# Six layers on one Trainium2 core: X transposes over two slots in the attentions, P^T kv in P's banks, expert slots in order of expert

## The reference

```python
x = norm(x + L0_attn(x))    # "gqa": rope over heads, 16 q heads, 4 kv heads, softmax, biases
x = norm(x + L0_xattn(x))   # "latent": 16 heads, scores over a 128-wide latent context
x = norm(x + L0_ffn(x))     # ternary weights, 512 -> 1408 -> 512, sigmoid gate
x = norm(x + L1_attn(x))    # "decay": linear attention in blocks, 16 heads, biases
x = norm(x + L1_xattn(x))   # "causal": keys and values from the 128-wide context, softmax
x = norm(x + L1_ffn(x))     # 8 experts, two chosen per token, and a shared expert

# L1_ffn
logits = x @ gate_weight.T
topk_w, topk_idx = top_k(softmax(logits), 2)
y[t] = sum over the two experts e of t:  topk_w * (down_e @ (silu(g) * u)),  (g, u) = gate_up_e @ x[t]
y += shared expert
```

## Time and profile before

| | |
|---|---|
| runs, median (lowest to highest) | 2352.07 us (2348.92 to 2352.67) |
| profiled execution, its own time | 2348.88 us |
| its span in the trace | 2347.1 us |
| mean granted clock of TensorE | 0.93 |
| busy: TensorE / DVE / ACT / POOL | 2015.7 / 1078.3 / 711.8 / 356.7 us |
| from the last expert matmul to the end | 70.6 us |

### The profile page before, as it was taken

One profiled execution on the slowest core, in us unless ns is written; L12 is line 12 of the kernel. 1 busy time (PEld: TensorE's weight loads), 2 busy tenths in 40 slices (PEclk: granted clock), 3 DMA queues, 4 the chain that ended last, 5 costly groups with the idle time before them and its releaser, 6 DMA issues. The chain is left out here.

```text
span 2347.1 us, 32879 instructions
## 1 busy us (share of the span) xinstructions
PE 2015.7 (86%) x12204; PEld 1636.4 (70%) x12204; DVE 1078.3 (46%) x1916; ACT 711.8 (30%) x2261; POOL 356.7 (15%) x317
## 2 busy tenths in 40 slices
PE   4899958889999978999789996899977999899970
PEld 3777636777777756777667774677756777799960
DVE  4466743344444436433344454566754232222226
ACT  1455623233333333111131101344532121233322
POOL 0111000000000007300021100000002300544216
PEclk9899968999999998999889997899987999999995
DMA  5011133000000004000150001000013200543226
GB/s 176 1 38 38 39 120 121 31 1 1 1 1 1 1 1 135 14 0 0 40 216 1 1 1 63 1 1 1 1 40 112 108 0 0 209 146 133 82 74 190
DMA packets 54284, 125.65 MB, mean 54 GB/s; under 512 B 5248, under 2 KB 23040, under 8 KB 51840
## 3 DMA queue, kind: packets, MB, share of 16 engines
q1 hardware_dynamic: 29088, 83.91, 10.2%
q0 software_dynamic: 5840, 27.92, 3.4%
q10 hardware_dynamic: 19216, 11.89, 1.8%
HBM read 90.68 MB, written 33.03 MB: 53 GB/s over the span
## 5 line engine op out<-in xcount | busy, mean ns | idle before, releaser
L1165 PE MATMUL banks<-ternary_xth,ternary_wq 128*128 (+1 forms) x352 | 138.5, 393 | 1.4 <-DVE ternary_xtl L73 1.4
L1165 PE MATMUL banks<-ternary_xtl,ternary_wq 128*128 (+1 forms) x352 | 138.3, 393 | 0.0
L388 ACT ACTIVATE causal_pr<-banks,causal_nb 128x128 f32<-128x128 f32 x256 | 90.1, 378 | 77.9 <-DVE causal_nb L511 77.9
L100 PE MATMUL banks<-latent_vh,latent_cth 128*128 128x512 f32 x256 | 104.3, 407 | 10.1 <-DVE latent_ctl L878 10.1
L388 ACT ACTIVATE gqa_pr<-banks,gqa_nb 128x128 f32<-128x128 f32 x256 | 90.1, 378 | 71.6 <-DVE gqa_nb L511 71.6
L555 PE MATMUL banks<-ident,X 128*128 128x128 f32 x192 | 36.9, 359 | 86.4 <-DVE gqa_xgl L485 32.1
L878 DVE TENSOR_TENSOR latent_ctl<-banks,latent_cth 128x512 fp32r<-128x512 f32 x64 | 44.3, 692 | 140.2 <-ACT latent_cth L819 140.2
L100 PE MATMUL banks<-weights,expert_xgh 128*128 x312 | 104.5, 335 | 2.4 <-DVE expert_xgl L1657 2.4
L102 PE MATMUL banks<-weights,expert_xgl 128*128 x312 | 101.2, 324 | 0.0
L101 PE MATMUL banks<-weights,expert_xgh 128*128 x312 | 101.1, 324 | 0.0
L102 PE MATMUL banks<-latent_vh,latent_ctl 128*128 128x512 f32 x256 | 100.2, 391 | 0.0
(11 more groups left out here) (420 smaller groups left out, 5699.4 us busy)
## 6 DMA issues: line engine op xcount, KB each, us to landing
x_slots<-decay_zeros SPq DMA_DIRECT2D x39, 256.0 KB, 2.9
expert_xin<-x_slots SPq DMA_DIRECT2D x39, 256.0 KB, 2.8
y_slots<-expert_ys SPq DMA_DIRECT2D x39, 256.0 KB, 2.1
weights_raw<-in_expert_experts SPq DMA_DIRECT2D x4, 2176.0 KB, 8.5
gqa_tw<-in_ternary_w ACTq DMA_DIRECT2D x4, 2112.0 KB, 10.6
ternary_raw<-in_ternary_w SPq DMA_DIRECT2D x11, 768.0 KB, 4.2
expert_raw<-in_expert_experts POOLq DMA_DIRECT2D x3, 2176.0 KB, 9.3
latent_qt<-in_latent_fold SPq DMA_DIRECT2D x6, 864.0 KB, 4.5
```

Source lines behind the costliest of these rows:

```text
L100: pe.matmul(out, wh, xh, start=first, stop=False, **kw)
L388: a = act.activation(pr[:, h, c, :], S.bank[2 * h + c // 4][:, (c % 4) * P:(c % 4 + 1) * P], ACT.Exp, bias=nb[:, h, c:c + 1], accum_out=su ...
L1165: a = pe.matmul(dst[:, :], wq[:, j, m, c * P:(c + 1) * P], x[:, c, toks], start=c == 0 and n == 0, stop=c == C - 1 and n == 1)
```

## The change

It has three parts.

1. **Attention.** The plan starts with X's transposes, and the q weights come after them. They are loaded and split in four chunks (`split_q`), and the first q product waits chunk by chunk. For gqa X's first four tiles come as four transfers, and q's chunks are loaded right behind them; for causal q's chunks stand ahead of the context. Of a group's four transposes the first two stand at the end of slot 7 of the group before, the other two in slot 0; causal's `c` stands in slot 1, behind q.
2. **Latent.** `ct0` and `ct1` go to banks 2 and 3, `cth` and `ctl` are doubled, and both stand together where `ct0` stood, ahead of `E1`.
3. **Experts.** Of a token's two slots the first is now that of the lower expert number. The gathers of the lower ones may begin when the tiles of expert 6 are stored; eight of them go into a buffer of eight rows that the loaded weights have left free. The rest follow in a ring of eight. The norm is made in five sets of tiles with one power for each, the output goes out in 16 transfers. `y_slots` is zeroed in the decay phase too.

The diff, cut to its core:

```diff
@@ attention_phase
-        heads = [("x", i) for i in range(GT)] + ([("c", 0)] if kind == "causal" else [])
+        xs = [("x", i) for i in range(GT)]
+        cx = [("c", 0)] if kind == "causal" else []
...
-            by_slot = [heads, qs[0:1], qs[1:2], qs[2:3], qs[3:4], ks, vs[0:2], vs[2:4]]
+        if soft:
+            by_slot = [xs[2:4], qs[0:1] + cx, qs[1:2], qs[2:3], qs[3:4], ks, vs[0:2], vs[2:4]]
         else:
-            by_slot = [heads, qs[0:2], qs[2:4], ks[0:2], ks[2:4], vs[0:2], vs[2:3], vs[3:4]]
-        plan = [(n, 0, i) for part in by_slot for n, i in part]
+            by_slot = [xs[2:4], qs[0:2], qs[2:4], ks[0:2], ks[2:4], vs[0:2], vs[2:3], vs[3:4]]
+        plan = [(n, 0, i) for part in [xs[0:2]] + by_slot for n, i in part] + [("x", 1, i) for i in range(2)]
...
+                if b < B - 2 * GT and 2 * (b % GT) + h == 2 * GT - 1:
+                    plan += [("x", b // GT + 2, i) for i in range(2)]
@@ sync
-                sp.dma_start(S.X[:, 0:GT, :], S.x_dram[:, 0:GT, :]).then_inc(x_in[0], 16)
+                for i in range(GT):
+                    sp.dma_start(S.X[:, i, :], S.x_dram[:, i, :]).then_inc(x0_in[i], 16)
+            for c in range(C):
+                sp.dma_start(ws[0][:, c * DM:(c + 1) * DM], w["q"][:, c, :]).then_inc(wq_in[c], 16)
...
-                    sp.dma_start(rows, zeros[:, :]).then_inc(slots_zero, 16)
+                    for slots in (S.x_slots, S.y_slots):
+                        rows = slots.rearrange("(i p) n -> i p n", p=P)[bass.ds(i, 1)].rearrange("o p n -> (o p) n")
+                        sp.dma_start(rows, zeros[:, :]).then_inc(slots_zero, 16)
@@ scalar
+            def split_q():
+                for c in range(C):
+                    ...
+                    act.activation(wqh[:, c, :], ws[0][:, c * DM:(c + 1) * DM], ACT.Copy).then_inc(wq_hi, 1)
@@ vector
+            def split_q():
+                if n_loads:
+                    dve.wait_ge(const_in, 16 * n_loads)
+                for c in range(C + 1):
+                    if c < C:
+                        dve.wait_ge(wq_in[c], 16)
+                        if kind == "gqa":
+                            rotate(0, [c])
+                    if c:
+                        dve.wait_ge(wq_hi, c)
+                        dve.tensor_tensor(wql[:, c - 1, :], ws[0][:, (c - 1) * DM:c * DM], f32(wqh[:, c - 1, :]),
+                                          ALU.subtract).then_inc(wq_lo, 1)
+                    if what == "q":
+                        split_q()
+                        if kind == "gqa":
+                            biases()
                     split("qkv".index(what) + 1)
@@ tensor
+                        if b == 0 and h == 0 and what == "q":
+                            pe.wait_ge(wq_lo, c + 1)
@@ latent_phase
-        cth, ctl = sb("cth", [P, N], F32R), sb("ctl", [P, N], F32R)
+        cth, ctl = sb("cth", [P, 2, N], F32R), sb("ctl", [P, 2, N], F32R)
-                plan.append(("ct0", *units[k - 1]))
+                plan += [("ct0", *units[k - 1]), ("ct1", *units[k - 1])]
...
-            if 0 <= k - 1 < len(units):
-                plan.append(("ct1", *units[k - 1]))
-        BANKED = ("x", "c", "q", "k", "fm", "fc", "fv", "ct0", "ct1")
+        BANKED = ("x", "c", "q", "k", "fm", "fc", "fv")
+                    act.wait_ge(ct_full, ct_of[e])
+                    if ct_of[e] > 2:
+                        act.wait_ge(out_done, ct_of[e] - 2)
+                    act.activation(cth[:, x, :], S.bank[2 + x], ACT.Copy).then_inc(ct_hi, 1)
...
                     pe.wait_ge(p_norm, u + 1)
                     if u:
-                        pe.wait_ge(pt_done, u)
+                        pe.wait_ge(ct_lo, 2 * u)
...
-                    wait_freed(pe, ("ct1" if x else "ct0", b, i))
+                    pe.wait_ge(ct_lo, 2 * turn[(b, i)] + x + 1)
@@ shared_ffn_phase
-            for dst, k in ((eq, 0), (lg, 1)):
-                rc.link(dve.tensor_tensor(dst[:, :, :], io, b8(ixf[:, :, k]), ALU.is_equal))
+            for dst, op in ((low, ALU.min), (high, ALU.max)):
+                a = dve.tensor_tensor(dst[:, :], ixf[:, :, 0], ixf[:, :, 1], op)
+            rc.link(a)
+            for dst, first in ((eq, low), (lg, high)):
+                a = dve.tensor_tensor(dst[:, :, :], io, b8(first[:, :]), ALU.is_equal)
+            rc.link(a)
-            dve.tensor_copy(S.score[:, :], m8[:, :, 0:2])
+            for dst, own in zip(weighed, (eq, lg)):        # behind w_lo
+                a = dve.tensor_tensor(dst[:, :, :], ex[:, :, :], own[:, :, :], ALU.mult)
+            rc.link(a)
+            for k, dst in enumerate(weighed):
+                dve.tensor_reduce(S.score[:, k * B:(k + 1) * B], dst[:, :, :], AX, ALU.add)
@@ expert_ffn_phase
+    NY = 8
+    sets = [(0, 4), (4, 8), (8, 12), (12, 14), (14, 16)]
-        yg = xin
+        yg = S.raw[:, 0:NY * DM].rearrange("p (n d) -> p n d", d=DM)
+            pool.wait_ge(w_ready, E)
+            landed(E - 2)        # y_copied >= last tile of expert 6, plus 2
+            for n in range(B):
+                if n >= NY:
+                    pool.wait_ge(low_added, n - NY + 1)
+                gather(n)
+            landed(E - 1)
+            for t in range(B):
+                if t < NY:
+                    pool.wait_ge(low_added, t + NY + 1)
+                else:
+                    pool.wait_ge(high_added, t - NY + 1)
+                gather(B + t)
+                if t >= NY and t % 4 == 3:
+                    norm(t // 4 - 2)
+            for k in range(2, len(sets)):
+                norm(k)
@@ expert_ffn_phase, vector, behind the tile loop
+            for t in range(B):
+                low(t)
+            ends = [hi - 1 for lo, hi in sets]
+            for n in range(B + 2):
+                if n < B:
+                    high(n)
+                if 1 <= n <= B:
+                    dve.wait_ge(high_added, n)
+                    dve.bn_stats(out=six[:, n - 1, :], in_=S.X[:, n - 1, :]).then_inc(six_done, 1)
+                if n >= 2:
+                    dve.wait_ge(six_done, n - 1)
+                    dve.bn_aggr(out=mv[:, n - 2, :], in_=six[:, n - 2, :]).then_inc(mv_done, 1)
+                    if n - 2 in ends:
+                        spread(ends.index(n - 2))
+                if n - 4 in ends:
+                    shifts(ends.index(n - 4))
```

More of the change, by code:

```diff
@@ L728, in latent_phase @@
         bank_no = {e: (place[e] % 6 if place[e] < len(first) else 4 + place[e] % 2) for e in banked}
+        cts = [e for e in plan if e[0] in ("ct0", "ct1")]
         ahead, latest = {}, {}
@@ L784, in wait_half_free @@
                 eng.wait_ge(pp_full, place[("k", b - 1, 3)] + 1)
-            if what in ("ct0", "ct1"):
-                n = 2 * turn[(b, i)] + int(what == "ct1")
-                if n:
-                    eng.wait_ge(out_done, n)
         blocks = ExitStack()
@@ L1694, in _ @@
+            for k in range(len(sets)):
+                if ends[k] + 4 >= B + 2:
+                    shifts(k)
         @block.tensor
```

198 lines of the change are left out of this document (107 added, 91 removed).

## The result

The changed kernel takes 2261.9 us, the median of four runs (2257.88 to 2267.6), against 2350.49 of the kernel before in the runs beside it: a ratio of 0.9629 (95% interval 0.9613 to 0.9645), 88.6 us less. Predicted were 2277 and 74.7 us less; the result lies in the range and nearer to its low end.

The account below looks back on a forecast made before the run. TensorE, busy 2015.7 of 2347.1 us, was taken to lose the rest mostly waiting for DVE, itself queued behind something. The terms summed to 74.7 us: 2352.07 - 74.7 = 2277 us, range 2256 to 2302.

Parts of the forecast that it names:

- 1a: Start of gqa: X's low halves made before the constants land, first bank read at 40.2; 2.5 us (0 to 6).
- 1b: Start of decay: low halves in chunks, first bank full at about 1180.8 instead of 1185.5; 4 us (2 to 7).
- 1c: Start of causal: q loaded ahead of the context, q1 starts at 1449.2 and not 1459.2; 8.3 us (5 to 12).
- 1d: X's transposes of later groups in the attentions: the stall moves more than it shrinks; 13.6 us (3 to 30).
- latent: Latent steps: most of PE's 33.5 us of waits for ctl go, 3 us taken off; 27 us (17 to 31).
- experts: Tail behind the expert tiles: early gathers, DVE then the bound, smaller last transfer; 20 us (15 to 24).
- others: Small added costs: score, low and high operations and ten more semaphores to clear in each attention; -0.7 us.
- I count no gain of clock: Later groups: the 3.8 us wait before out is still followed by the lower clock level, so nothing comes back.
- rival D: Early gathers disturb the last five expert tiles; 1 us a tile costs 5: 2282, inside the range; 0.71 together with the sum.
- A: Rival: the waits move on, latent's chain is longer and slots 7 and 0 give nothing; gain 42, 2310; chance 0.15.
- B: Rival: all waits go, the clock no longer falls at the groups; gain 95 to 100, 2255; chance 0.07.
- C: Rival, slower: latent closes a loop of more than 14.15 us a step; at 17.5, +30, 2380; chance 0.05.

Follow-up runs that it names:

- x_in_slot0: The changed kernel with all four X transposes of a group back in slot 0, none in slot 7; 2263.91 us.
- c_in_slot0: The changed kernel with all four X transposes and also causal's c back in slot 0, c ahead of q at the start too; 2282.46 us.
- the three parts alone: The kernel before with only the attention, latent or expert part of the diff: 30.2, 35.0 and 21.0 us less than the kernel before.
- experts_only: The kernel before with the expert part of the change alone; 2327.5 us, ratio 0.9909.
- attention_only: The kernel before with the attention part of the change alone, y_slots not zeroed; 2318.2 us, ratio 0.9859.
- x_at_slot_ends: The changed kernel with X's transposes in gqa and causal at slot ends, behind pv of slot 7 and rt of slot 0; 2245.07 us, ratio 0.9558.

## Why the prediction was right, and where not

The gain by stages, as means over the profiles that share the code of a stage, against the terms of the sum:

| term | forecast | measured | from |
|---|---|---|---|
| 1a gqa's start | 2.5 | 5.7 | gqa 320.1 to 314.9 is 5.2, the two later boundaries cost 0.5 |
| 1b decay's start | 4 | 2.9 | 269.5 to 266.6 (x_in_slot0, c_in_slot0) |
| 1c causal's start | 8.3 | 9.8 | 306.1 to 301.8 (c_in_slot0) is 4.3, and 5.5 for c behind q |
| 1d later groups | 13.6 | 8.0 | gqa -0.5, decay 2.5, causal's X -4.1, its c 15.6 less the 5.5 of its start |
| latent | 27 | 36.5 | 560.4 to 523.9 (520.3 to 527.3) |
| experts | 20 | 20.5 | tiles and tail, 340.0 to 319.5 |
| others | -0.7 | 2.8 | shared, 265.9 to 263.1, by the clock |
| sum | 74.7 | 86.2 | the medians say 88.6, the three parts alone 86.2 |

The time lies in the stated range, but the terms are not all right: latent and gqa's start gave 12.7 us more than forecast and the later groups 5.6 less, so a part of the agreement is errors that offset each other.

- **Latent** is the term that was mis-sized, by 9.5 us. The mechanism was as told: the waits fell from 33.5 to 3.5 us, and `ct1` fills `out0`'s wait. Three us were taken off for a chain over ACT and DVE that might be late at T; it never is, in the 22 steps TensorE is busy without a break. And a wait costs more than the idle time the profile writes down: in the cycle 3.1 us of waits, three in number, went and 3.72 us came back, so 0.2 us each beyond the idle time. Most of that is the overlap: a matmul of 512 columns is shown with 0.39 us but begins 0.23 us behind the one ahead, and behind a wait the 0.16 us don't overlap. The 0.50 us of the first matmul behind a wait is no part of it, for the first of a group shows it without a wait too (the row at 574.86 above). For some 25 waits 0.2 us make 5, an estimate: 30.0 + 5 for the forecast 29.9 - 3. The last 1.5 us of the 36.5 are within the spread of the profiles (520.3 to 527.3).
- **1a**: the reckoning of DVE's queue held (POOL's disturbance 3.4 us for 4), but its start was taken from before: the constants at 18.05. They land by 15.2; with whole transfers by 17.9, and the bank is then read at 39.5. The edit was charged "nothing" for the loads, where it changed who stands ahead of whom. The lower clock at q2 did not come either: TensorE had not been idle for 5 us, since q0's chunks wait one by one and run at the lower clock themselves, and q2 waits 1.02 us.
- **1b**: 2.9 for 4, inside its bounds. The doubled zero writes cost nothing to be seen: decay takes 269.4 us with them in experts_only and 269.4 without them before, and in the new order 263.7 without (attention_only) and 263.8 to 264.6 with them.
- **1c** held, q1 12.3 us behind the start for 13. 5.5 us of the stage hang on `c` standing behind q.
- **1d**: the place and size of the new waits were right (0.81 and 3.65 in gqa, 1.50 and 3.65 in causal, for 1.0 and 3.8), the gain wasn't. The step that failed is the one on the clock, "I count no gain of clock": it left out that there could be a loss. In gqa `out` came 1.4 us sooner, as forecast (1.2), but the lower level that follows the wait now falls on `out`'s twelve matmuls, which begin 0.43 us apart instead of 0.23 and take 1.6 to 1.7 us longer than with all four transposes in slot 0. In causal the waits in slot 7 are longer (0.34 and 1.50), so `out` came no sooner, and only `c` gained. The Trainium skill (TensorE: Matmul & The Clock Gate, section HAM oscillation) says that the clock falls again when TensorE sits idle between bursts, and this trace agrees with it, at 3.65 us of idle time here and at 4.53 before. A slip besides: gqa's own parts (1.2 twice and 1.4) make 3.8, not the 3.5 of the sum.
- **Experts** held nearly to the microsecond, a tail of 50.4 us for 50.3, though partly by chance: POOL and DVE take turns in being late (3.5 us for powers, 6.0 for gathers), and the eight early gathers disturb the tiles by 0.7 us (rival D had 5).
- **Rivals**: A's stall that moves on came true in the attentions and nowhere else; B's vanishing waits in latent and nowhere else, and its clock that stays up is what x_at_slot_ends shows. C's loop never closed: the cycle is what TensorE's own work takes.

## What to carry to other kernels

Where two tasks share banks in a fixed order, a task that waits is helped only by what stands *between* the bank's last reader and it: ask for each entry which queue its reader stands in, and put entries whose readers are late behind those that are needed at once; dealing them over two slots moved the stall, putting them behind `out` took 17 to 20 us off the time. Price a wait of TensorE at its idle time plus a restart (0.2 us here), and where the lower clock follows it, ask how much work stands behind the wait: `out` came 1.4 us sooner and lost it again, because its twelve matmuls were what stood behind the wait. Early transfers by the dozen beside a running stage are not free: eight gathers cost 0.7 us and saved 14, sixteen cost 12 and saved 9 more.

## What the runs showed of the hardware that was not expected

- During sixteen indirect gathers of 256 KB in a row ACT stood still for 13.59 us and TensorE paused between matmuls with nothing due. The cause stays open. That the engines' instructions came late behind the gathers was not tested, and the trace lends it no support: from 2189 to 2216 us it has no packet of the DMA queues of kind "instruction", and ACT went on at 2208.39 without one.
- The same instructions at the head of the shared stage were granted a mean clock of 0.67 in one execution and 0.89 in another; the stage was between 259.9 and 266.8 us. Gains under some 7 us in one stage are not shown by one pair of profiles.
- DVE's 128x512 operation on two SBUF operands took 1.63 us while POOL added rows of X, and 0.69 otherwise; POOL's four rows took 5.73 us together, 1.43 each, for 1.24 each in the earlier trace rows.
